# Gated cross-attention and linear-feature attention on one core: key rows packed as 64 + 13 per head instead of end to end

## What is computed

```python
f_q, f_k, f_v = (proj(q), proj(k), proj(v))          # layer_norm(t) @ w_in.T, split into 8 heads
cosine_sim = dots / (qn[..., :, None] * kn[..., None, :])
var_component = einsum('hqn,hqm->hqnm', q_ratio, k_ratio)
mixed = cw * cosine_sim + vw * (cosine_sim * decorr_scale) + ww * var_component
out = einsum('hqnm,hqmd->hqnd', mixed, f_v)          # then heads joined, @ w_out.T + b_out
```

## Time and profile before

| | |
|---|---|
| median of three executions | 1363.93 us |
| the profiled execution, its own time | 1365.88 us |
| its span, first to last instruction | 1364.4 us |
| mean granted TensorE clock | 0.978 |
| busy: PE, PE weight loads | 1259.7 us (92%), 799.1 us (59%) |
| busy: DVE, ACT, POOL | 1113.5 us (82%), 1026.6 us (75%), 191.5 us (14%) |
| chain that ended last | PE 60%, DVE 14%, issue 11% |
| one full turn (from one F4 to the next) | 71.0 us |

### The profile page before, as it was taken

The page is one execution under the profiler, slowest core; times in us unless marked ns, Lnnn a source line. Parts: engine busy times, 40 slices in busy tenths (PEclk is TensorE's granted clock), DMA queues, the critical chain, the costliest instruction groups (busy, mean ns, idle before and its releaser), DMA issues.

```text
span 1364.4 us, 35000 instructions
## 1 busy us (share of the span) xinstructions
PE 1259.7 (92%) x10770; PEld 799.1 (59%) x10770; DVE 1113.5 (82%) x3164; ACT 1026.6 (75%) x3398; POOL 191.5 (14%) x130
## 2 busy tenths in 40 slices
PE   4999788999999999999999999999999999999864
PEld 2667556666656565657575657565656566665521
DVE  6986656897979797979797979798989889797854
ACT  5766233687878797979697979787888878787886
POOL 2352120102020202020100101010101020202000
PEclk9999899999999999999999999999999999999977
DMA  8440011606050515151414232332415060605140
GB/s 256 146 145 19 11 35 39 206 5 207 16 193 30 173 49 169 54 169 54 159 63 129 94 122 101 98 125 76 147 52 171 22 200 1 210 13 176 34 155 16
DMA packets 163127, 141.25 MB, mean 104 GB/s; under 512 B 9326, under 2 KB 150799, under 8 KB 163088
## 3 DMA queue, kind: packets, MB, share of 16 engines
q1 hardware_dynamic: 163088, 140.76, 31.8%
...
## 4 chain that ended last, share of the span: by engine, by line
PE 60%; DVE 14%; issue 11%; ACT 1%; POOL 1%; DVEq 0%; ACTq 0%; POOLq 0%; PEldq 0%
PE work L893 16%; PE work L895 15%; PE work L894 15%; PE attended L1393 8%; PE score L1382 4%; DVE nm L1674 4%; PE work L1285 2%; DVE Vpl L1571 2%; DVE l2s L1643 1%; DVE x2S L1637 1%; DVE xTl L1590 1%; DVE wqTl L1576 1%; DVE qst L1596 1%; PE work L1332 1%; ACT oTh L1488 0%
## 5 line engine op out<-in xcount | busy, mean ns | idle before, releaser
L1481 ACT ACTIVATE prob<-score,nm 128x256 f32<-128x256 f32 x1024 | 477.5, 499 | 41.9 <-DVE nm L1674 41.0
L1674 DVE TENSOR_REDUCE nm<-score 128x2 f32<-128x512 f32 x512 | 337.4, 681 | 11.1 <-PE score L1382 10.8
L1481 ACT ACTIVATION_READ_ACCUMULATOR prob<-score,nm 128x1 f32 x1024 | 238.6, 233 | 0.0
L1596 DVE BATCH_NORM_STATS2 qst<-work 128x6 f32<-128x128 f32 x512 | 112.5, 284 | 94.0 <-PE work L895 94.0
L1393 PE MATMUL attended<-prob,vsp 128*32 128x256 f32 x2048 | 138.9, 396 | 14.2 <-DVE vsp L1689 12.9
L1382 PE MATMUL score<-qstack,kstack 64*128 64x256 f16 x1024 | 99.7, 279 | 15.6 <-ACT prob L1481 13.5
L1528 POOL TENSOR_TENSOR rq<-qft,mhalf 128x32 f32<-128x32 f32 x16 | 86.8, 5427 | 164.4 <-DVEq L1603 164.4
L893 PE MATMUL work<-woutTh,fvph 128*128 128x256 f16 x384 | 105.2, 274 | 2.1 <-DVE Vpl L1571 1.1
L894 PE MATMUL work<-woutTl,fvph 128*128 128x256 f16 x384 | 104.7, 273 | 0.0
L895 PE MATMUL work<-woutTh,fvpl 128*128 128x256 f16 x384 | 104.7, 273 | 0.0
L893 PE MATMUL work<-wTh,xTh 128*128 128x512 f16 x256 | 97.5, 381 | 2.0 <-DVE xTl L1590 2.0
...
## 6 DMA issues: line engine op xcount, KB each, us to landing
qstack<-parts SPq DMA_DIRECT2D x64, 256.0 KB, 3.6
kstack<-parts SPq DMA_DIRECT2D x64, 256.0 KB, 4.1
...
parts<-qh SPq DMA_DIRECT2D x32, 256.0 KB, 2.4
parts<-ql SPq DMA_DIRECT2D x32, 256.0 KB, 2.5
```

The source lines that it names most:

```text
L1481: nc.scalar.activation(prob[:, g % PG, e, j + jj, :], sc[n % SC][:, jj * NQ:(jj + 1) * NQ], ACT.Exp, bias=nm[:, u + jj:u + jj + 1], accum_ ...
L1596: last = nc.vector.bn_stats(qst[:, t, 4 * half + h, :], bank(e)[:, h * DH:(h + 1) * DH])
L1674: nc.vector.tensor_reduce(nm[:, u:u + 2], sc[n % SC][:, :].rearrange("p (u q) -> p u q", q=NQ), AX.X, ALU.max, negate=True).then_inc(max_r ...
```

## The change

The 616 key rows of a batch element are laid out differently. Tiles 0 to 3 each hold 64 keys of two heads (rows 0 to 63 the even head, 64 to 127 the odd head). The 13 keys left of each head (`LEFT`) go to tile 4, in four quarters of 32 rows, each for one pair of heads.

- `V`: each head is multiplied once with 64 stationary columns into its half of a tile (6 matmuls a tile), and the rest with 32 columns into its quarter (24 matmuls). Per batch element 48 instructions instead of 36. Columns no longer wanted for windows shrink the padding (`FS`).
- `d`: the stationary side of tiles 0 to 3 is two pieces of 64 columns, that of tile 4 four of 32: per batch element 72 instructions instead of 30.
- `G`: 8 banks (`G0` to `G7`) of two heads instead of 6 of three, three and two; the matmuls are the same 48.
- `y`: the rows for the second factor and the constant leave the tiles for mE and vE of 73 rows, multiplied by one more matmul: 16 instead of 15 for each of four accumulations.
- `a0`: DVE writes every factor column 16 times (auxq, 512 elements instead of 32), the transposes give 128 rows at once, and ACT drains them straight into tile 4 of sqE. Only 8 transfers of 64 rows are left for tiles 0 to 3. `a1`: ACT writes two copies, the two transfers `wq` go, `ldr` has three transfers for two.
- POOL clears a few more tiles at the start.
- `ORDER` is another list throughout; `res` now stands ahead of `back1`, and `back1`, `out`, `back2` are last.

```diff
-PAD = 127 + MK
-PADW = 2 * H * PAD + 127
+LEFT = MK - 64
+FS, GS = 96, 80
+LO_ROW, LL_ROW = 32, 64
+Y_ROWS = LL_ROW + H + 1
...
+rk S0 S1 M0 V0 M1 V1 X0 qs1 V0.h V1.h X1 V0.l a1 qpow M2 a1.h G0 V1.l G0.h X2 a1.l G1 S2 M3 G1.h V2 G0.l X3 G1.l G2 M4
...
+zT1 X19 m5.l P3 M20 zT0.f M21 S11 zT1.h R4 y1 M22 E1 zT0.l L1 zT1.f y0.o X20 M23 zT1.l X21 O0 y1.o X22 ln1 S12 P4 X23
+O0. S13 M24 fk2 lpow M25 q0 fk2.h ln2 X24 X25 fk2.l zz0 q0.o zz1 zz0.h S14 M26 zz1.h q1 R5 X26 zz0.l P5 zz1.l M27 pq0
...
+pq1.l O1 E3 L3 pk1.l O2 O1. O3 O2. q2 O3. back0 q3 F1 q2.o parts1 pv0 q3.o F2 q4 pv0.v q5 q4.o F3 q6 q5.o back3 q7
+q6.o pv1 q7.o F4 pv1.v res back1 out back2
...
+def value_block(h, b2):
+
+    return FS * (2 * h + b2) + LEFT * (h % 2)
+
+
+def left_block(h, b2):
+
+    return FS * (2 * h + b2) + (64 if h % 2 == 0 else -16)
...
+    def key_tile(t, b2):
+
+        if t == HT - 1:
+            return [(32 * j, 32, GS * (4 * j + 2 * b2) + 64) for j in range(H // 2)]
+        return [(64 * odd, 64, GS * (4 * t + 2 * b2 + odd) + LEFT * odd) for odd in range(2)]
...
-                        heads = tile_heads(t)
-                        for h in heads:
-                            last = products(nc, bk[:, n * DIM:(n + 1) * DIM],
-                                            fvp, (ALL, slice(window(t, h, b2), window(t, h, b2) + P)),
-                                            w["woutT"], (ALL, h), h == heads[0], h == heads[-1])
+                        cols = slice(n * DIM, (n + 1) * DIM)
+                        if t < HT - 1:
+                            for m, (x, y) in enumerate(("hh", "hl", "lh")):
+                                for h in (2 * t, 2 * t + 1):
+                                    at = value_block(h, b2)
+                                    last = nc.tensor.matmul(bk[64 * (h % 2):64 * (h % 2) + 64, cols], fvp[x][:, at:at + 64],
+                                                            w["woutT"][y][:, h, :], start=m == 0, stop=m == 2)
+                            continue
+                        for odd in range(2):
+                            for m, (x, y) in enumerate(("hh", "hl", "lh")):
+                                for j in range(H // 2):
+                                    at = left_block(2 * j + odd, b2)
+                                    last = nc.tensor.matmul(bk[32 * j:32 * j + 32, cols], fvp[x][:, at:at + 32],
+                                                            w["woutT"][y][:, 2 * j + odd, :], start=odd == 0 and m == 0,
+                                                            stop=odd == 1 and m == 2)
...
-                            last = products(nc, bk[0:r, n * 2 * P:(n + 1) * 2 * P],
-                                            G, (ALL, k, slice(b2 * HM + t * P, b2 * HM + t * P + r)),
-                                            xT, (ALL, k, slice(b2 * NQ, (b2 + 1) * NQ)), k == 0, k == KT - 1)
+                            for m, (x, y) in enumerate(("hh", "hl", "lh")):
+                                for row, size, at in key_tile(t, b2):
+                                    last = nc.tensor.matmul(bk[row:row + size, n * 2 * P:(n + 1) * 2 * P], G[x][:, k, at:at + size],
+                                                            xT[y][:, k, b2 * NQ:(b2 + 1) * NQ], start=k == 0 and m == 0,
+                                                            stop=k == KT - 1 and m == 2)
...
-            return (G[half][:, c // 3, :].rearrange("p (b n) -> p b n", b=2)[:, :, lo_h * MK:hi_h * MK],
-                    bk[:, 0:(hi_h - lo_h) * PM].rearrange("p (b n) -> p b n", b=2), 1.0 / WS)
+            j = c % 4
+            return (G[half][:, c // 4, :].rearrange("p (n c) -> p n c", c=GS)[:, 4 * j:4 * j + 4, 0:MK],
+                    bk[:, 0:2 * PM].rearrange("p (n m) -> p n m", m=MK), 1.0 / WS)
...
+                        last = nc.tensor.matmul(bk[:, r * DIM:(r + 1) * DIM],
+                                                mE[0:Y_ROWS, c * NQ + r * P:c * NQ + (r + 1) * P], vE[0:Y_ROWS, c, :],
+                                                start=False, stop=True)
...
-                    drain(nc.scalar.activation(sqT[:], bank(e)[0:H, :], ACT.Copy), e)
+                    wait_drained(act, a - 1, "d5")
+                    drain(nc.scalar.activation(sqE[:, HT - 1, :], bank(e)[:, :], ACT.Copy), e)
...
-                    nc.scalar.activation(wqT["h"][:], bank(e)[0:H, :], ACT.Copy, scale=MS).then_inc(hi_ready[lead(e)], 1)
+                    nc.scalar.activation(mE[0:H, :], bank(e)[0:H, :], ACT.Copy, scale=MS)
+                    nc.scalar.activation(mE[LL_ROW:LL_ROW + H, :], bank(e)[0:H, :], ACT.Copy, scale=MS).then_inc(hi_ready[lead(e)], 1)
...
-                    nc.vector.tensor_tensor(aux[:, 0, :, :], rq[:], bc(w["cvec"][:].unsqueeze(1), [P, PT, H]),
+                    nc.vector.tensor_tensor(auxq[:].rearrange("p t (h i) -> p t h i", h=H), bc(rq[:].unsqueeze(3), [P, PT, H, 16]),
+                                            bc(w["cvec"][:].unsqueeze(1).unsqueeze(3), [P, PT, H, 16]),
                                             ALU.mult).then_inc(sq_ready, 1)
```

More of the change, by code:

```diff
@@ L41 @@
 HM_TILES = [(0, 1), (2, 3), (4,)]
[L42 to L45, removed]
 SB = NB // NG
@@ L954 @@
 ORDER = """
[L955 to L964, removed]
+rk S0 S1 M0 V0 M1 V1 X0 qs1 V0.h V1.h X1 V0.l a1 qpow M2 a1.h G0 V1.l G0.h X2 a1.l G1 S2 M3 G1.h V2 G0.l X3 G1.l G2 M4
+G4 V2.h S3 M5 G2.h G4.h V2.l X4 qs2 G2.l a0 G4.l X5 G3 R0 V3 M6 a0.v S4 M7 G3.h G5 aux V3.h P0 G3.l ldy M8 G5.h ldx X6
+V3.l G6 G6.h G5.l V4 X7 M9 V5 G6.l sqe0 V4.h R1 S5 G7 X8 M10 P1 V4.l G7.h V5.h G7.l fk0 X9 V5.l z S6 fk0.h d0 sqe1 X10
+M11 fk0.l X11 fk1 ldr M12 d0.o S7 fk1.h d1 M13 E0 X12 R2 fk1.l d2 m0.h L0 d3 X13 M14 m0.l X14 d1.o P2 d2.o m1.h M15 d4
+m2.h m1.l X15 m2.l d5 d3.o d4.o S8 m3.h S9 zT0 M16 m4.h y0 m3.l zT0.h M17 X16 d5.o M18 X17 R3 m5.h M19 X18 m4.l S10
+zT1 X19 m5.l P3 M20 zT0.f M21 S11 zT1.h R4 y1 M22 E1 zT0.l L1 zT1.f y0.o X20 M23 zT1.l X21 O0 y1.o X22 ln1 S12 P4 X23
+O0. S13 M24 fk2 lpow M25 q0 fk2.h ln2 X24 X25 fk2.l zz0 q0.o zz1 zz0.h S14 M26 zz1.h q1 R5 X26 zz0.l P5 zz1.l M27 pq0
+M28 X27 q1.o pk0 E2 X28 M29 R6 S15 pq0.h pq1 M30 X29 pq0.l X30 M31 pk1 L2 X31 P6 pk0.h R7 pk1.h pk0.l P7 pq1.h parts0
+pq1.l O1 E3 L3 pk1.l O2 O1. O3 O2. q2 O3. back0 q3 F1 q2.o parts1 pv0 q3.o F2 q4 pv0.v q5 q4.o F3 q6 q5.o back3 q7
+q6.o pv1 q7.o F4 pv1.v res back1 out back2
 """.split()
@@ L996, in half @@
     return group, e, 2 * i, 2 * (4 * group + 2 * e + i)
[L999 to L1008, removed]
+def value_block(h, b2):
+    return FS * (2 * h + b2) + LEFT * (h % 2)
+def left_block(h, b2):
+    return FS * (2 * h + b2) + (64 if h % 2 == 0 else -16)
+SQ_LOADS = [4, 4]
 def main_phase(nc, ctx, w, x_rows, out_rows, rk_rows, kr_rows, sq_rows, fixed_rows, parts):
@@ L1030, in main_phase @@
     rk_all, rkc = sb("rk_all", [P, HT, NB]), sb("rkc", [P, HT, 2])
-    aux, sqT, wqT = sb("aux", [P, 2, PT, H]), sb("sqT", [H, PR]), pair("wqT", [H, PR])
+    aux, auxq = sb("aux", [P, PT, H]), sb("auxq", [P, PT, P])
     st4, qst, qft = sb("st4", [P, PT, 2]), sb("qst", [P, PT, H, 6]), sb("qft", [P, 5, PT, H])
@@ L1331, in a_part @@
                     for t in range(PT):
-                        last = nc.tensor.transpose(bk[0:H, t * P:(t + 1) * P], aux[:, c, t, :], ident[:])
+                        if c == 0:
+                            last = nc.tensor.transpose(bk[:, t * P:(t + 1) * P], auxq[:, t, :], ident[:])
+                        else:
+                            last = nc.tensor.transpose(bk[0:H, t * P:(t + 1) * P], aux[:, t, :], ident[:])
                 elif kind == "y":
```

122 lines of the change are left out of this document (65 added, 57 removed).

## The result

The changed kernel takes 1416.83 us (median, 1416.61 to 1417.66), the kernel before, timed beside it, 1364.84 us (1363.42 to 1369.82): a ratio of 1.037, 95% interval 1.0344 to 1.0396. The direction was forecast, the size was not: 1374 us was said, 1388 was the end of the range. The profiled executions have spans of 1414.9 and 1364.4 us, so 50.5 us are to be explained.

A forecast was written before the change was run, and what follows sets the result against it. Bound: DVE from F4 to ln2, then PE from zz0 to q7, then q7.o. 0.72 + 0.20 + 0.1 - 0.25 = +0.8 us over 14 turns, +11, with -1 for turn 1, gave 1374 us; range 1360 to 1388.

The forecast's parts named there:

- list: head: DVE before ln2: xTl of zT1 moves ahead of ln2, +0.60 us a turn; R5 moves behind it, -0.52.
- list: tail: TensorE from zz0 to q7: q0 out, S14 and P5 in, +0.20 us; pq0 waiting for drains, +0.1.
- layout: DVE before ln2: auxq of 512 elements instead of 32, +0.50 us; eight G drains, +0.14, a turn.
- waits won back: DVE from F4 to ln2: an early PE removes some of 0.6 us of waits, taken as -0.25 a turn.
- up to the first F4: Turn 1: V's saving shows partly, taken as -1 us; new POOL clears and small transfers at the start, 0 to +2.
- the ring: Whole turn: DVE from F4 to ln2, about 45.8 us, plus PE from zz0 to q7, 24.4, plus q7.o, 0.8.
- I cost it at nothing: First part of the turn: PE loses 2.6 us a pair, which turns into waits for drained banks and gains nothing.
- Rival A: PE's saving comes through: each turn 2.6 us shorter, -37, so 1327 us; chance 0.10.
- Rival B: No measurable change: 1365 us, or 1360 if auxq also costs less than an xTl; chance 0.24.
- Rival C: 64-wide tiles in V and d don't overlap: +3 us a turn, +42, so 1406 us; chance 0.06.
- D: New wait on a transfer: back1 lands later than S4 could start, 14 us for each microsecond; chance 0.04.
- ACT "covered, thinly": ACT in the first part: two more G drains and a second a1 copy, about 1 us a turn, hidden.

The follow-up runs named there:

- run 1: Kernel before with only 18 instead of 36 of V's matmuls per batch element issued, nothing else changed: 1372.15 us, ratio 1.0038.
- run 6: Kernel before, its tiles, factors and code kept, with the changed kernel's list (G6 and G7 dropped, wq behind V5): 1403.59 us, ratio 1.0258.
- run 5: Changed kernel with 20 useless filler matmuls on PE in step a1, ahead of its wait for aux: 1414.45 us (1408.13 to 1423.23).
- run 3: Changed kernel with ldx, the load of the next x, moved to behind V1 and res moved behind out: 1412.90 us.
- run 4: Changed kernel with one ScalarE copy for a1 instead of two: 1415.14 us.
- run 7: Changed kernel's tiles, factors and code with the old list, G6 and G7 put between V4 and d0, V5 behind G7: 1427.21 us, ratio 1.0435.

## Why the prediction was wrong

The accounts, per clean turn and in all:

| part | forecast | measured |
|---|---|---|
| list: head (xTl +0.60, R5 -0.52) | +0.08 | +1.10 |
| list: tail (0.20 and pq0 0.1) | +0.30 | +0.44 |
| layout (auxq 0.50, G 0.14) | +0.64 | +1.11 |
| waits won back | -0.25 | none |
| half clock | not in it | +0.45, mean |
| waits for x | not in it | +0.22, mean |
| 13 turns | +10 | +43.1 |
| up to the first F4 | -1, start 0 to +2 | +7.5 |

**The step that failed** is "Of each part only what stands on the ring's own engine counts", with DVE "without rest" from F4 to ln2. The shares had warned: PE 43.91 of 45.96 beside DVE's 44.13. What the runs show instead is two engines that are both nearly full and take turns on the path. Work taken from PE in V gives nothing (run 1: 71.02 us), but work added to PE costs most of itself (y 0.30 of 0.44; pv0 at least 1.15 for 1.31). "I cost it at nothing" was right for V's saving and wrong for what PE gets: V lies in large part in the first stretch, where drains set the pace in the old list, y's slots in the middle one, where PE has no pause. V's saving of 3.9 us didn't pay for y. The forecast took DVE's wait of 0.4 us in the earlier trace rows for time to be won; it is the place where the path comes over from PE.

The sum of the reordering failed beside it, and by more: in the head the list costs 1.10 us where 0.08 was said, with the old tiles and PE's old work (run 6). That is shown; by which waits it comes is not. The forecast added the steps that cross ln2 and took every other reordering as free. The three rows of each kernel above show how it divides on DVE: it is busy 43.99 us in the head before, 44.31 in run 6 and 45.40 in run 5, and idle 1.82, 2.60 and 2.62. The list came mostly as pauses. The layout came as DVE's busy time, 1.09 for 0.64; as an operation with a pause behind it counts about 0.08 us longer (0.68 from start to end, 0.60 from start to start), a part of this isn't work. For the layout the ring over DVE is not refuted: auxq's 0.49 came as said, y's 0.30 was missing, and the last 0.3 of the 1.11 aren't taken apart.

**The clock** wasn't in the forecast at all. It is for the most part a second effect of PE's saving: with V halved and nothing else changed 12 of 13 turns have it (run 1), with the new list and V at its old length 3 of 13 (run 6), before none. At a pause (2.5 us at a1; at most 1.5 us in run 1) and shortly behind it the granted clock is 0.50, and matmuls of V, G and S take up to twice as long (rounds of V's quarters 0.216 us apart instead of 0.109). The Trainium skill, page "TensorE: Matmul & The Clock Gate", section "A second HAM failure mode: psum-queue depth-cycling", says that short idles of PE between groups of matmuls, as it goes round its PSUM banks, make the clock swing; runs 1 and 5 agree, with a price of 0.67 us a turn in run 1 and of 0.45 in the changed kernel.

**Rival A** fell for the reason given against it: run 1 gave nothing. **Rival B** fell, since the change is far outside the noise. **Rival C** fell: V's pairs start together, two rows of V (x2 is a pair, the next starts 0.11 us later) being

```profile
699.93 0.28 PE L1327 MATMUL work<-woutTl,fvph 128*64 128x256 f16 x2
700.04 0.28 PE L1327 MATMUL work<-woutTh,fvpl 128*64 128x256 f16 x2
```

and 24 of d's matmuls take 1.43 us, 12 slots of 0.109 and a change of form. **D** came in small and elsewhere: no wait on back1, but z waited for x, 0.5 us a turn, and run 3 shows that it cost 0.2. **auxq** took 0.68 us, as said. **The waits won back** fell: oTl's 11.4 us over 13 turns went (5.5 of them in the heads), and others of over 20 us came in the heads. **ACT "covered, thinly"**: not quite, up to 0.3 us a turn by run 4.

**What stays open**: the 7.5 us ahead of the first F4 (7.0 come with the list alone in run 6, 4.9 with the layout on the old list in run 7, 5.4 are left in run 5), which waits make up the list's 1.10 us in the head, and why run 5's other executions are up to 15 us longer than the profiled one.
